# A degree count shared between VectorE and GpSimd, and its first block loaded in four parts

## What is computed

```python
h = jnp.maximum(_layernorm(x, axis=-1), 0.0)
x = x + _L0_gnn_ref(h, L0_gnn_W, L0_gnn_b, src, dst)

def _L0_gnn_ref(feature, W, b, src, dst):
    n = feature.shape[0]
    agg = jax.ops.segment_sum(feature[src], dst, num_segments=n)
    deg = jax.ops.segment_sum(jnp.ones_like(dst, dtype=feature.dtype), dst, num_segments=n)
    mean_h = agg / jnp.maximum(deg, 1.0)[:, None]
    h = jnp.where(deg[:, None] > 0, mean_h, feature)
    return jax.nn.relu(h @ W.T + b)
```

## Time and profile before

| | us |
|---|---|
| median of 3 runs | 5279.04 (5275.83 to 5281.31) |
| the profiled execution, its time | 5277.98 |
| its span | 5275.9 |
| VectorE busy in the span | 4374.3 (83%) |
| TensorE matmuls busy | 3320.8 (63%) |
| GpSimd busy | 3130.6 (59%) |

### The profile page before, as it was taken

How to read it: one execution, slowest core, us unless ns; L and a number is a source line. 1 busy time by engine, 2 the same in 40 slices (tenths; PEclk the granted TensorE clock), 3 DMA queues, 4 the chain that set the end, 5 groups by cost and what they waited for, 6 DMA issues and landing times.

```text
span 5275.9 us, 65740 instructions
## 1 busy us (share of the span) xinstructions
PE 3320.8 (63%) x13965; PEld 1555.5 (29%) x13965; DVE 4374.3 (83%) x14057; ACT 3173.8 (60%) x10162; POOL 3130.6 (59%) x3140
## 2 busy tenths in 40 slices
PE   4555578677777657777764777777343433336799
PEld 1111134333333233333322333333221111113444
DVE  7999989699999869999996999999788888885211
ACT  5666610677777557777764777777377777770100
POOL 3444400677777677777776777777377777771000
PEclk9999997788988778888886989898767667678899
DMA  4333362344444434444442444444267777772466
GB/s 140 131 131 131 131 246 95 86 128 128 127 122 129 120 82 129 127 123 127 129 123 68 128 129 129 123 126 129 60 244 278 281 280 282 280 279 64 177 234 224
DMA packets 324085, 817.57 MB, mean 155 GB/s; under 512 B 71032, under 2 KB 238948, under 8 KB 308904
## 3 DMA queue, kind: packets, MB, share of 16 engines
q1 hardware_dynamic: 225336, 605.05, 31.1%
q0 software_dynamic: 95024, 206.12, 16.4%
q10 hardware_dynamic: 3392, 2.75, 0.2%
HBM read 352.28 MB, written 461.40 MB: 154 GB/s over the span
## 4 chain that ended last, share of the span: by engine, by line
DVE 33%; POOL 18%; issue 11%; PE 11%; ACT 8%; DMA 6%; POOLq 0%; DVEq 0%; SPq 0%; ACTq 0%
POOL big L631 17%; DVE big L1606 8%; DVE big L1523 7%; PE psT L934 6%; DMA big<-table,src_win 4%; DVE big L1596 4%; DVE big L1546 2%; ACT hT L792 2%; DVE big L1616 2%; PE psY L1141 1%; DVE lane_x L1374 1%; DMA big<-A_d 1%; POOL big L645 1%; ACT hT L798 1%; ACT hT L807 1%
## 5 line engine op out<-in xcount | busy, mean ns | idle before, releaser
L631 POOL DMA_INDIRECT big<-table,src_win x2744 | 2647.8, 965 | 894.6 <-issue 798.6
L1054 PE MATMUL psY<-big,hT 128*128 128x420 bf16 x4200 | 1080.6, 405 | 725.0 <-ACT hT L798 724.1
L792 ACT ACTIVATE hT<-src_bc,node_c 128x128 bf16<-128x128 f16 x4200 | 1289.9, 386 | 63.2 <-DMA src_bc<-pe_src_d 54.2
L1606 DVE SCALAR_TENSOR_TENSOR big<-big,keep_win 128x132 f32<-128x132 f32 x2184 | 782.4, 358 | 77.8
L1054 PEld LDWEIGHTS psY<-big,hT 128*128 128x128 bf16 x4200 | 408.2, 110 | 1388.1 <-ACT hT L798 618.2
L1523 DVE TENSOR_SCALAR big<-src_bc,node_c 128x128 bf16<-128x128 f16 x4200 | 714.0, 284 | 0.6 <-issue 0.5
L1082 PE MATMUL psS<-big,hT 128*128 128x384 bf16 x1400 | 353.1, 430 | 549.4 <-DVE hT L1533 549.4
L798 ACT ACTIVATE hT<-hT 128x640 bf16<-128x640 bf16 x840 | 589.3, 720 | 0.0
L590 POOL TENSOR_SCALAR big<-big 128x400 bf16<-128x400 f16 x198 | 285.1, 1440 | 356.6 <-PE psY L993 166.8
L823 ACT ACTIVATE psH<-d_b 128x60 f32<-128x60 f32 x168 | 37.6, 224 | 695.2 <-DVE d_b L1588 695.2
L1060 PE MATMUL psL<-big 128*128 128x420 bf16 x2100 | 395.0, 344 | 18.1 <-DVE big L1523 15.6
(11 more groups left out here) (327 smaller groups left out, 5381.8 us busy)
## 6 DMA issues: line engine op xcount, KB each, us to landing
rows<-big SPq DMA_DIRECT2D x112, 1792.0 KB
rows<-big SPq DMA_DIRECT2D x168, 952.0 KB
big<-A_d SPq DMA_DIRECT2D x18, 6400.0 KB, 19.8
A_d<-big SPq DMA_DIRECT2D x396, 200.0 KB, 1.9
big<-table,src_win POOLq DMA_INDIRECT x2744
src_bc<-pe_src_d SPq DMA_DIRECT2D x168, 64.0 KB
table<-big SPq DMA_DIRECT2D x15, 350.0 KB
big<-A_d SPq DMA_DIRECT2D x3, 1600.0 KB, 6.9
```

The lines of the kernel that those rows point to most:

```text
L631: pool.indirect_dma_start(out=rows[:, k, 0:p.table_w], out_offset=None, in_=table, in_offset=bass.IndirectOffsetOnAxis(ap=src_win[:, s, k: ...
L792: ins = nc.scalar.activation(is_src[:, t, P:P + n], src_bc[:, s % 2, P:P + n], ACT.Square, bias=node_c[:, t:t + 1], scale=-1.0)
L1054: ins = nc.tensor.matmul(psF[0][s % 2][:, 0:3 * p.table_w], is_src[:, t, 0:P], table_s[:, t, :, :].rearrange("p c w -> p (c w)"), start=(t ...
L1606: v.scalar_tensor_tensor(state[:, k, 0:GATW], prev[k][:, 0:GATW], kw[:, 0, k:k + 1], rows[:, k, 0:GATW], ALU.mult, ALU.add).then_inc(chain ...
```

## The change

VectorE reduces over the first 17 source tiles only. GpSimd adds up the other eight (`POOL_S`), in seven instructions a block, into a new view `some` of `dst_i`, a tile that is no longer read by then; each waits for the one before. VectorE adds `some` to its own sum before it counts `red_rdy`. GpSimd starts a block when it has landed and VectorE has used the previous `some`. SP's loads from block 2 on wait for GpSimd's reads too. Block 0 is loaded by four DMAs of 8 tiles (1600 KB) in place of one, with semaphores of their own for the first three, and VectorE reduces it in four instructions, each after its part has landed; TensorE and GpSimd wait for all parts.

```diff
+POOL_S = 8
+PARTS = 4
...
+        some = dst_i[:].bitcast(F32)[:, 0:DENSE_T * W]
...
+        a_part = [sem(f"a_part{i}") for i in range(PARTS - 1)]
+        part_sum = sem("part_sum")
...
                 if m == 0 and b >= 2:
+                    sp.wait_ge(part_sum, (POOL_S - 1) * (b - 1))
                     sp.wait_ge(red_rdy, b - 1)
...
             sp.wait_ge(zero_in, 16)
-            for b in range(NBK):
+            n = DENSE_T // PARTS
+            for i in range(PARTS):
+                sp.dma_start(abuf[1][:, n * i:n * i + n, :], A_d[n * i:n * i + n, :, :].rearrange("b p q -> p b q")
+                             ).then_inc(a_part[i] if i < PARTS - 1 else a_in[1], 16)
+            for b in range(1, NBK):
                 load_counts(0, b)
...
+            pool.wait_ge(lanes_rdy, 2)
+            for b in range(NBK):
+                n = blocks[b][1]
+                pool.wait_ge(a_in[(b + 1) % 2], 16 * (b // 2 + 1))
+                if b == 0:
+                    for i in range(PARTS - 1):
+                        pool.wait_ge(a_part[i], 16)
+                else:
+
+                    pool.wait_ge(red_rdy, b)
+                to = some[:, 0:n * W].rearrange("p (b w) -> p b w", w=W)
+                a = abuf[(b + 1) % 2]
+                frm = [a[:, 0:n, W * k:W * k + W] for k in range(NT - POOL_S, NT)]
+                pool.tensor_tensor(to, frm[0], frm[1], ALU.add).then_inc(part_sum, 1)
+                for k in range(2, POOL_S):
+                    pool.wait_ge(part_sum, (POOL_S - 1) * b + k - 1)
+                    pool.tensor_tensor(to, to, frm[k], ALU.add).then_inc(part_sum, 1)
...
                 pe.wait_ge(a_in[(at + 1) % 2], 16 * (at // 2 + 1))
+                if at == 0:
+                    for i in range(PARTS - 1):
+                        pe.wait_ge(a_part[i], 16)
...
             def degrees(b):
 
                 n = blocks[b][1]
-                dve.wait_ge(a_in[(b + 1) % 2], 16 * (b // 2 + 1))
                 if b >= 2:
                     dve.wait_ge(deg_ps, b - 1)
-                v.reduce_sum(reds[b % 2][:, 0:n * W].rearrange("p (b w) -> p b w", w=W),
-                             abuf[(b + 1) % 2][:, 0:n, :].rearrange("p b (s w) -> p b w s", w=W),
-                             mybir.AxisListType.X).then_inc(red_rdy, 1)
+                k = n // PARTS if b == 0 else n
+                for i in range(n // k):
+                    if b == 0 and i < PARTS - 1:
+                        dve.wait_ge(a_part[i], 16)
+                    else:
+                        dve.wait_ge(a_in[(b + 1) % 2], 16 * (b // 2 + 1))
+                    ins = v.reduce_sum(reds[b % 2][:, k * i * W:k * (i + 1) * W].rearrange("p (b w) -> p b w", w=W),
+                                       abuf[(b + 1) % 2][:, k * i:k * (i + 1), 0:W * (NT - POOL_S)].rearrange(
+                                           "p b (s w) -> p b w s", w=W), mybir.AxisListType.X)
+                link(ins)
+                dve.wait_ge(part_sum, (POOL_S - 1) * (b + 1))
+                v.tensor_tensor(reds[b % 2][:, 0:n * W], reds[b % 2][:, 0:n * W], some[:, 0:n * W], ALU.add).then_inc(red_rdy, 1)
```

## The result

The changed kernel takes 5257.81 us (median of 6 runs, 5255.41 to 5260.07); the kernel before, run beside it, 5277.07 us (6 runs, 5274.55 to 5281.31). The ratio is 0.9963, 95% interval 0.9951 to 0.9975: 19.3 us less, where 27 were forecast. The profiled execution's span went from 5275.9 to 5253.7 us.

A forecast was written before the change was run, and what follows sets the result against it. VectorE's loop (34.95 us a block) was taken to bound blocks 2 to 5, with TensorE's 26.65 as floor. 137.26 - 4 x 27.8 = 26.1, + 1.4 - 0.4 = 27.1 us saved: 5252.0 us; 8-in-10 range 5244 to 5271.

The forecast's parts named there:

- the contention: GpSimd's additions beside VectorE's segments and outputs: seven delays, 1.8 us a block, between 0 and 12.6; VectorE's loop 27.8 us.
- The reduction over 17 tiles: VectorE's reduction in each block: time goes by elements, 14.8 us, saving 7.0 us a block; 17.5 us as bound.
- rival 1: VectorE's reduction has a price per output: 17.5 us, loop 30.5 us, time 5264 us; chance 0.09.
- Block 0's parts: Block 0 loaded and reduced in four parts: gain 0, as TensorE waits for all; last landing 0.4 us later.
- VectorE's addition: VectorE adding GpSimd's sum to its own in each block: 0.75 us with the two waits before it.
- GpSimd's additions: Seven on GpSimd each block: 1.80 us each, between 0.55 and 3.6; done in time, so their length costs nothing itself.
- rival 2: Between VectorE's reductions, it and GpSimd exclude each other for whole instructions: 9.8 us a block, 5284 us, no change; chance 0.12.
- my own sign (over 1 us longer): VectorE's segment and output instructions: a few tenths longer beside GpSimd as forecast; over 1 us longer means rival 2.
- Rival 4: Blocks 2 to 5: no contention, TensorE sets the pace at 26.65 us, 5247.5 us; a third of the forecast's chance.
- The granted clock: TensorE in blocks 2 to 5: gaps stay short, so the clock is kept at 1.0.
- Block 1's period: Between the starts of TensorE's neighbour sums for blocks 1 and 2: TensorE's own pace, unchanged at 26.65 us.
- The last block: End of the pass: shorter reduction (5.57 to 3.79 us) less the addition saves 1.4 us of 23.39.

The follow-up runs named there:

- Experiment 2: Changed kernel with GpSimd's seven additions a block replaced by fills that only write (computation incomplete); ratio 0.9947 to the kernel before on a slower chip, pass 200.1 us.
- experiment 1: Changed kernel with GpSimd's additions from block 2 on also waiting for VectorE's last output tile of block b-2; rerun 5243.25 us, ratio 0.9943 to the kernel before.
- experiments 3 and 4: Kernel before plus only block 0's four parts, ratio 0.9995; changed kernel without the parts, ratio 0.9998; both against the kernel before on a slower chip.
- experiment 6: Changed kernel with GpSimd's seven additions made twice, 14 a block; 5258.26 us, ratio 0.9968 to the kernel before, pass 217.2 us.

## Why the prediction was right, and where its sizes were off

The direction, the place and the range for 8 in 10 held; 8 us of the forecast gain did not come. That 5257.81 us still lies inside my narrower 5245 to 5258 is luck: the periods of blocks 2 to 5 were to be 27 to 28.5 us and were 28.9, 30.9, 30.8 and 28.4, and the contention was not of the size that I had taken.

- *The reduction over 17 tiles* was forecast at 14.8 us: 14.88. It goes by elements, and rival 1 is out. Block 0's parts took 3.79 us each (3.7 forecast). *VectorE's addition* took 0.69, with the wait in front of it 0.72 (0.75 forecast).
- *GpSimd's additions* were put between 0.55 and 3.6 us, 1.80 taken: 1.27, and 1.35 from start to start. The figure of the Trainium skill ("GPSIMD Engine Reference", Elementwise — side-by-side cycle accounting) gave an estimate of 1.12, nearer than mine by elements from L590. Their length was to cost nothing by itself, and it did not.
- *The contention* is the term that was mis-sized: 1.8 us a block taken, 4.4 measured in block 2, VectorE's loop 30.4 to 30.8 us and not 27.8. I took L590's 0.26 us as the price per GpSimd instruction. The rule of the Trainium skill ("SBUF — State Buffer", Who interferes with whom), which I set aside, describes what happened: L1434 took its own 0.75 us and 0.89 more, most of an addition of 1.27. By rival 2's own working, additions of 1.27 us, 1.35 from start to start, come to some 6 us (0.2 for the rest of the second, then five turns of 1.2), where 4.4 were measured: L1433 waited for nothing, and a turn cost 0.9 to 1.1 us. So it was rival 2's mechanism at a smaller price that ran, and by my own sign (over 1 us longer) L1437 and L1439, 1.07 and 1.06 us longer, say so. L590 differs from the additions in having one f16 input and not two f32; why it holds L1295 for so much less than its 1.41 us no run here settles. Experiment 2 shows that the reads are the part that holds L1434.
- *Rival 4*, TensorE's own pace, is what experiment 1 gives: 26.57 us, with the contention moved away.
- *The granted clock* was to stay at 1.00: it was 0.89 to 0.98, since TensorE now waited up to 4.60 us for output tiles. After that wait L980 takes 0.79 and not 0.49 us, and a neighbour sum 23.5 us. It costs where TensorE sets the pace: in block 5 some 1.9 us, and 0.5 us in the last output tile of block 1's period. In experiment 1, without the contention, it is 1.00 in blocks 2 to 5 (every sum 21.62 us).
- *Block 1's period* was taken as unchanged, and grew by 1.6 us: GpSimd starts block 2 when its load lands, at 751.03, and is then beside block 0's output tiles (L1453 at 758.09 took 1.07 us, the next 0.66): TensorE waits 1.15 us more for them, and the lower clock behind that is the other 0.5. I had placed the additions only behind `red_rdy`.
- *Block 0's parts* gain 0, as forecast (experiments 3 and 4); the delay of the last landing is 0.43 us for 0.4. The last block gives 1.35 us for 1.4. SP's wait cost nothing.

Together: 18.3 + 1.35 gained in blocks 2 to 5 and at the end, 0.6 in block 0 (25.6 for 26.2; its neighbour sum took 24.08 us and not 24.67, without the parts 24.09, so no part of the change is seen to do it), less 1.6 and 0.43, is 18.2 us of pass, of 19.3 measured between the medians.

## What to carry to other kernels

When work goes from VectorE to GpSimd, ask which VectorE instructions it will lie beside, not only whether it is done in time. Beside a reduction with one input seven additions cost 0.1 us; beside a stretch of short two-input and one-input elementwise instructions they cost 4.4 us a block, more than half of the 7 us that they took off VectorE. One more wait, which starts them later, gave back 13 us. And a load in parts helps only where the engine that sets the pace uses the parts.

## What the runs showed of the hardware

- VectorE and GpSimd take turns where VectorE reads two SBUF tiles, or runs a one-input `TENSOR_SCALAR`, beside GpSimd's additions: L1434 went from 0.75 to 1.64 us, L1439 (128x4) from 0.17 to 1.23, and six additions from 7.98 to 8.85. L1451 and L1452, which read one SBUF tile and one of PSUM, kept their 0.35 us, and a reduction beside seven additions took 14.97 us for 14.88. A GpSimd fill holds a `TENSOR_SCALAR` (0.48 to 0.84) but not L1434.
- Such an instruction waits only for the rest of the addition in progress: 0.18 to 0.38 us where 0.7 us of other work lies between two such instructions (experiment 6).
- A reduction from SBUF with its innermost step at 64 bytes takes 1.7 ns an element whether it has 17 or 25 of them per output; L1546 from PSUM takes 1.4 with all its fixed part.
- TensorE's neighbour sum took 21.62 us behind gaps of 2.04 and 0.26 us in the output tiles (at 790.48), and 23.5 us behind one of 4.60 (at 821.33), with the granted clock at 0.50 until 825 and 1.00 from 827 on.
